# Dense products of 512 columns put into each slot of the first three attentions of a vision tower

## The chip, the cores and the metric

The kernel runs on one core of one Trainium2 chip. The metric is the device time of one execution in microseconds (us). The kernel before was timed three times: 1929.55 us is the median, 1923.34 us the lowest and 1930.13 us the highest.

## The reference, cut to what matters

32 images become 37 tokens each (36 patches and a class token) of 192 numbers. Then come seven attentions with 12 heads and five feed-forward layers, three of which send tokens to experts. The change touches the first three attentions alone, which have heads of 16 numbers. Each computes, in float32,

```
qkv = xn @ qkv_w.T                       # q, k, v: [B, 12, 37, 16]
attn = q @ k^T * scale                   # first: minus 0.2 * sum of its 8 neighbours; second: causal mask
out = softmax(attn) @ v                  # third: the diagonal is masked
h = layernorm(h + out [@ w_proj + ...])  # the first has no output projection
```

None of these values changes.

## The kernel before, in words

The 32 images are taken in 11 groups of three (`G = 11`, 111 tokens: `TG`). A program in Python (`PROGRAM`) lists steps of all stages in one order, and each engine walks the same list and does its part of each step; so the order of work on each engine is written out by hand. The stages are: attention `NEIGH`, attention `CAUSAL`, an expert layer, attention `DIAG`, then four times a wider attention (`T5`) and a feed-forward layer.

The first three attentions have `short` set. Their order comes from `short_order` (and `short_fill`, which places the small jobs): slot n of an attention holds, in this order,

- S(n): scores of group n on TensorE (`att_step`, kind "S", L1058 to L1090). First PE waits until both score banks of the slot before have been taken by VectorE. In `CAUSAL` and `DIAG` a bfloat16 product puts the mask into each bank (L1074). Then come 12 products (24 in `NEIGH`, which adds those of the neighbour sums) of 37 columns over 64 rows (L1085). In the profile a float32 product is two instructions.
- OT(n-2): the attention output of group n-2 is turned (L1140), into a projection bank, after a wait until VectorE has divided it. `NEIGH` has no OT.
- PT(n-1): the probabilities of group n-1 are turned into `ps_pt` (`turn_prob`, L992 to L1000), after waits until ScalarE has made their exponentials and has taken the turned ones of the group before.
- Y(n-2): output projection (L1157). `NEIGH` has XA in its place, which is no work of TensorE.
- E(n), exponentials, on ScalarE; PV(n-1): probabilities times values (L1119), 12 products of 51 columns.
- in between: projections QK of a later block of groups (L1034), V of the next group (L1048; in `NEIGH` also a product of one row, L1053), turns A of normalised rows (L977, in `DIAG` L971 and L973), tokens TOK (L1015), and for the follower the expert logits L (L1174) and counts CNT (L1182, L1183).

QK, V and A steps of kind fp32r (`w1_hi`, `w1_lo`, `xa_hi`, ...) run in one instruction per product. The weights of each stage lie in `w1_hi`, a ring of three slots (`W_RING`); attention a's are in slot `LOAD0[("att", a)] % W_RING`. ScalarE rounds a new load into a slot at a step W1 (L1362), after the last projection that reads the slot's old content.

VectorE (DVE) does the softmax's maximum and shift (L1550, L1552), the division (L1561, L1564), residual additions and the start of each norm; GpSimd (POOL) does the rest of the norm (L1417 to L1460) and the DMAs of rows to and from the experts (L1385); ScalarE (ACT) does exponentials and most evictions (L1332, L1338, L1310), and in `NEIGH` it spreads the queries by head (QS, L1247), which S of a block's first group waits for.

Of the kernel before, what the change touches and what calls it, by code (L numbers as in the profile page):

```python
# [25 lines left out]
G = -(-B // IPG)  # L26
# [26 lines left out]
NEIGH, CAUSAL, DIAG, T5 = 0, 1, 2, 3  # L53
# [26 lines left out]
ATTS = [Att(a) for a in range(NATT)]  # L80
# [48 lines left out]
LOADS, LOAD0 = [], {}  # L129
# [454 lines left out]
W_RING = 3  # L584
# [3 lines left out]
def tower(nc, patches, tok_w, consts, young, rows, gains, gates_w, head_scale, bias_src, wo_all, w1_all, w2_all, out, rows_in, rows_out):  # L588
    with ExitStack() as ctx:
# [29 lines left out]
        w1_hi = sb("w1_hi", [128, W_RING, 2, F], F32R)  # L619
# [68 lines left out]
        ps_pt = ps("ps_pt", [128, 512])  # L688
# [249 lines left out]
        def _(pe):  # L938
# [53 lines left out]
            def turn_prob(a, g, u):  # L992
                n = unit(a, g, u)
                pe.wait_ge(prob_ready, n + 1)
                if n:
                    pe.wait_ge(pt_taken, n)
                for i in range(4 if ATTS[a].short else 3):
                    src = short_ring(prob, n)[:, i * TG:(i + 1) * TG] if ATTS[a].short else prob[:, n % 4, i, :]
                    last = pe.transpose(ps_pt[0:TG, i * TG:(i + 1) * TG], src, ident)  # L999
                last.then_inc(pt_full, 1)  # L1000

            def att_step(st, step):
                a = st[1]
# [3 lines left out]
                kind, g = step[0], step[1]  # L1007
# [3 lines left out]
                elif kind == "TOK":  # L1011
                    bank = proj_bank(key)
# [5 lines left out]
                elif kind == "QK":  # L1018
                    _, b, j = step
# [36 lines left out]
                elif kind == "S":  # L1056
                    p = step[2]
                    banks = [score_bank((*key, e)) for e in range(2)]  # L1058
                    b = BLOCK_OF[g]
                    if g == BLOCKS[b][0] and p == 0:  # L1060

                        for j in (s.qk - 2, s.qk - 1):
                            proj_out((st, "QK", b, j))
                        if a == NEIGH:

                            pe.wait_ge(qs_ready, 4 * (b + 1))
                            pe.wait_ge(band_done, 2 * (b + 1))
                    t0 = (g - BLOCKS[b][0]) * TP
                    if s.short:
                        if SCORE[(*key, 0)] % 2:  # L1070
                            banks.reverse()
                        for bank in banks:
                            if a != NEIGH:
                                pe.matmul(bank[0:TG, 0:2 * TG], identb[:],  # L1074
                                          maskb[:, a, 0:2, :].rearrange("p h k -> p (h k)"),
                                          start=True, stop=False, skip_group_check=True)
                        parts = [(short_q(b % 2), short_k(b % 2))]
                        if a == NEIGH:
                            parts.append((qband[:, b % 2, :, :, :, :], neigh_kb(b % 2)))
                        for j in range(2):  # L1080
                            for i in range(IPG):
                                for part, (q_t, k_t) in enumerate(parts):
                                    for e, bank in enumerate(banks):
                                        at, col = 64 * e, (j * IPG + i) * NTOK
                                        ins = pe.matmul(bank[0:TG, col:col + NTOK],  # L1085
                                                        q_t[at:at + 64, j, g - BLOCKS[b][0], i, :],
                                                        k_t[at:at + 64, j, t0 + i * NTOK:t0 + (i + 1) * NTOK],
                                                        start=(a == NEIGH and part == 0),
                                                        stop=(part == len(parts) - 1), skip_group_check=True)
                                        if (j, i, part) == (1, IPG - 1, len(parts) - 1):  # L1090
                                            ins.then_inc(score_full, 1)
                        return
                    for i in range(3):
                        for e, bank in enumerate(banks):
                            c, at = s.heads(2 * p + e)[i]
                            ins = pe.matmul(bank[0:TG, i * TG:(i + 1) * TG],  # L1096
                                            qk[at:at + 64, b % 2, c, t0:t0 + TG],
                                            qk[at:at + 64, b % 2, s.chunks + c, t0:t0 + TG],
                                            start=True, stop=True, skip_group_check=True)
                            if i == 2:  # L1100
                                ins.then_inc(score_full, 1)
                elif kind == "PT":
                    turn_prob(a, g, step[2])
                elif kind == "PV":
                    p = step[2]
                    n = OUT_AT[(a, g, p)]
                    pe.wait_ge(pt_taken, unit(a, g, 0 if s.short else 2 * p + 1) + 1)
                    pe.wait_ge(o_ready, OUT_AT[(a, g - 1, p)] + 1 if s.t5 and g else n)
                    if p == 0 or s.short:
                        for j in range(s.vparts):  # L1110
                            proj_out((st, "V", g, j))
                    if s.short:
                        turned_p = short_ring(probt, unit(a, g, 0))
                        wide = VWIDE // H
                        for h in range(H):

                            at = (h // 3 % 2 * 2 + h // 6) * TG + h % 3 * NTOK
                            col = h % 6 * wide
                            last = pe.matmul(ps_o[0:NTOK, h // 6, col:col + wide], turned_p[:, at:at + NTOK],  # L1119
                                             vimg[:, g % 2, h * wide:(h + 1) * wide], start=True, stop=True,  # L1120
                                             skip_group_check=True)
                        last.then_inc(o_full, 1)
                        return
                    for e in range(2):
                        u = 2 * p + e
                        for i, (c, at) in enumerate(s.heads(u)):
                            h = s.head(c, at)
                            col = (h % 6) * (s.d + 1)
                            last = pe.matmul(ps_o[0:TG, h // 6, col:col + s.d + 1], probt[:, unit(a, g, u) % 4, i, :],  # L1129
                                             v64[:, g % 3, h, :], start=True, stop=True, skip_group_check=True)  # L1130
                    last.then_inc(o_full, 1)
                elif kind == "OT":
                    bank = proj_bank(key)
                    j = step[2]
                    pe.wait_ge(o_ready, OUT_AT[(a, g, j if s.t5 else 1)] + 1)
                    if s.short:
                        for c, n in ((0, 128), (1, 64)):
                            for i in range(IPG):
                                at = c * TG + i * NTOK
                                last = pe.transpose(bank[0:n, at:at + NTOK],  # L1140
                                                    o[0:NTOK, g % 2, i * C + c * 128:i * C + c * 128 + n],
                                                    ident[0:NTOK, 0:NTOK])
                    else:
                        for i in range(3):
                            c = 3 * j + i
                            last = pe.transpose(bank[:, i * TG:(i + 1) * TG], o[:, g % 2, c * 128:(c + 1) * 128], ident)
                    last.then_inc(proj_full, 1)
                elif kind == "Y":
                    bank = proj_bank(key)
                    for j in range(s.vparts):  # L1150
                        proj_out((st, "OT", g, j))
                    if g == 0:
                        pe.wait_ge(wo_in, 16 * a)
                    w = wo[:].rearrange("p (c n) -> p c n", c=FC)
                    parts = [(c, 128) for c in range(6)] if s.t5 else [(0, 128), (1, 64)]
                    for c, n in parts:
                        last = pe.matmul(bank[0:TG, 0:C], ot[0:n, g % 2, c, :], w[0:n, c, :],  # L1157
                                         start=(c == 0), stop=(c == len(parts) - 1))
                    last.then_inc(proj_full, 1)
# [846 lines left out]
```

## Time and profile before

| what | value |
|---|---|
| median of three runs | 1929.55 us |
| the profiled execution's own time | 1929.32 us |
| its span, first to last instruction | 1927.5 us |
| mean granted TensorE clock over the span | 0.855 |
| `NEIGH`, first scores to `CAUSAL`'s first scores | 52.6 to 195.3 us |
| `CAUSAL`, second slot to last slot's scores | 207.8 to 302.2 us |
| `DIAG`, second slot to last slot's scores | 486.2 to 581.0 us |

The granted clock is a share of full speed: TensorE runs at 2.4 GHz where it is 1.00 and at 1.2 GHz where it is 0.50; a stretch with a value between had both. Times in the views are counted from the start of the span. A slot runs from one group's scores to the next group's.

### The profile page before, as it was taken

The numbers are of one execution on the slowest core, as the hardware profiler recorded it, in microseconds if no ns is written. First come the engines' busy times: TensorE is split into PE (matmuls) and PEld (weight loads), VectorE is DVE, ScalarE is ACT, GpSimd is POOL, SyncE is SP. The second block draws the span as 40 slices with busy tenths as digits, with TensorE's granted clock in tenths as the row PEclk, the third lists the DMA queues.
The fourth block names the chain that finished last, engine by engine and source line by source line (L and its number), as shares of the span: only waits on it lengthen the run. The fifth ranks groups of instructions, "written<-read, shape, count | busy, mean of one in ns | idle before, by whom it ended". The sixth has DMA issues, their size and how long they took to land.

```text
span 1927.5 us, 33597 instructions
## 1 busy us (share of the span) xinstructions
PE 1611.0 (84%) x11901; PEld 1489.6 (77%) x11901; DVE 1066.9 (55%) x2975; ACT 776.8 (40%) x1843; POOL 549.6 (29%) x1292
## 2 busy tenths in 40 slices
PE   5888798793989998999978999588989998899970
PEld 5777676792777997988878889588888987788960
DVE  4564457232655676567764343377755668434436
ACT  1433432341343553454433444244534544254420
POOL 2244335004754112612340000453234123300030
PEclk8765766896577998999888999879989989899995
DMA  4120101451069000100014666200010000256630
GB/s 143 33 73 10 43 17 38 126 164 56 26 202 275 30 2 17 62 2 6 16 34 147 213 196 198 71 15 1 1 62 18 1 16 15 63 184 209 204 91 28
DMA packets 78393, 149.75 MB, mean 78 GB/s; under 512 B 6340, under 2 KB 57843, under 8 KB 78230
## 3 DMA queue, kind: packets, MB, share of 16 engines
q1 hardware_dynamic: 71894, 135.35, 21.9%
q0 software_dynamic: 6336, 12.26, 2.2%
q8 instruction: 98, 1.61, 0.4%
q14 instruction: 65, 0.53, 0.1%
HBM read 106.59 MB, written 41.05 MB: 77 GB/s over the span
## 4 chain that ended last, share of the span: by engine, by line
PE 51%; issue 18%; DVE 15%; DMA 6%; ACT 5%; POOL 3%; SPq 1%; another core or an unknown queue 0%; DVEq 0%; POOLq 0%; ACTq 0%
PE ps_proj L1034 10%; PE ps_proj L1157 5%; PE ps_score L1228 5%; PE ps_proj L1048 5%; PE ps_o L1129 4%; PE ps_pt L999 4%; DMA w_in<-w_all_dram 4%; PE ps_proj L1211 4%; PE ps_score L1085 3%; PE ps_score L1096 3%; PE ps_o L1119 3%; ACT w_hi L1362 2%; PE ps_proj L1015 1%; DVE prob L1536 1%; DVE w_lo L1697 1%
## 5 line engine op out<-in xcount | busy, mean ns | idle before, releaser
L1228 PE MATMUL ps_score<-w,hid 128*112 128x192 f32 (+2 forms) x1680 | 305.1, 334 | 8.9 <-DVE x L1847 8.9
L1228 PEld LDWEIGHTS ps_score<-w,hid 128*112 128x112 f32 (+2 forms) x1680 | 277.0, 180 | 11.3 <-DVE x L1847 10.8
L1352 ACT ACTIVATE hid<-ps_proj 128x224 f32<-128x224 f32 (+2 forms) x360 | 133.6, 382 | 265.7 <-PE ps_proj L1211 258.9
L1440 POOL TENSOR_SCALAR tmp<-rs,var 111x1 f32<-111x1 f32 x110 | 40.9, 372 | 583.8 <-DVE rs L1510 583.0
L1401 POOL DMA_INDIRECT tin<-rows_out,idx x66 | 68.1, 1032 | 484.9 <-issue 379.9
L999 PE MATMUL ps_pt<-const,prob 111*111 111x111 f32 x660 | 129.3, 315 | 34.2 <-ACT probt L1340 22.4
L1157 PE MATMUL ps_proj<-wo,ot 128*111 128x192 f32 (+1 forms) x616 | 138.9, 375 | 4.0 <-ACT ot L1318 3.7
L999 PEld LDWEIGHTS ps_pt<-const,prob 111*111 111x111 f32 x660 | 96.2, 205 | 55.0 <-issue 27.2
L1340 ACT ACTIVATE probt<-ps_pt 111x333 f32<-111x333 f32 x176 | 78.9, 448 | 131.1 <-PE ps_pt L999 130.5
L1129 PEld LDWEIGHTS ps_o<-v,probt 111*111 111x111 f32 x1056 | 128.9, 195 | 0.5
L1332 ACT ACTIVATE prob<-prob 111x333 f32<-111x333 f32 (+1 forms) x209 | 102.6, 493 | 58.6 <-DVE prob L1539 40.0
L1129 PE MATMUL ps_o<-v,probt 111*111 111x65 f32 x1056 | 125.6, 274 | 0.0
L1157 PEld LDWEIGHTS ps_proj<-wo,ot 128*111 128x111 f32 (+1 forms) x616 | 112.1, 203 | 15.1 <-issue 12.3
L1211 PE MATMUL ps_proj<-ta_hi,w_hi 128*128 128x224 f32 (+1 forms) x264 | 94.6, 358 | 28.6 <-ACT hid L1352 23.4
L1362 ACT ACTIVATE w_hi<-w_in 128x1536 fp32r<-128x1536 f32 x65 | 96.4, 1483 | 54.3 <-DMA w_in<-w_all_dram 54.3
L1255 ACT ACTIVATE xa_hi<-ps_turn,gainf 128x111 fp32r<-128x111 f32 x132 | 46.5, 352 | 175.7 <-PE ps_turn L977 121.9
L1285 ACT ACTIVATE qk<-ps_proj 128x336 f32<-128x336 f32 (+1 forms) x192 | 82.3, 429 | 82.6 <-PE ps_proj L1034 80.2
L1536 DVE TENSOR_TENSOR prob<-ps_score,relbias 111x333 f32<-111x333 f32 x176 | 88.8, 505 | 41.6 <-PE ps_score L1096 35.8
L1697 DVE TENSOR_TENSOR w_lo<-w_in,w_hi 128x768 fp32r<-128x768 f32 x65 | 62.3, 959 | 88.1 <-ACT w_hi L1362 87.8
L1034 PE MATMUL ps_proj<-xa_hi,w_hi 128*128 128x336 f32 (+1 forms) x240 | 91.1, 380 | 11.7 <-DVE xb L1677 8.6
L977 PE MATMUL ps_turn<-const,xn 111*128 111x111 f32 x242 | 52.1, 303 | 55.8 <-POOL xn L1460 25.7
L1539 DVE TENSOR_TENSOR prob<-prob,negmax 111x333 f32<-111x333 f32 x176 | 89.9, 511 | 6.0
(250 smaller groups left out, 4172.1 us busy)
## 6 DMA issues: line engine op xcount, KB each, us to landing
w_in<-w_all_dram SPq DMA_DIRECT2D x65, 768.0 KB, 4.3
w<-w_all_dram SPq DMA_DIRECT2D x50, 576.0 KB, 5.0
rows_in<-zero SPq DMA_DIRECT2D x1, 12320.0 KB, 47.8
rows_out<-zero SPq DMA_DIRECT2D x1, 9240.0 KB, 80.5
tin<-rows_in SPq DMA_DIRECT2D x36, 224.0 KB
rows_out<-tout SPq DMA_DIRECT2D x36, 168.0 KB
patch<-patches_dram SPq DMA_DIRECT2D x11, 333.0 KB, 3.0
wo<-wo_all_dram SPq DMA_DIRECT2D x6, 576.0 KB, 3.8
```

Of the source, the lines that this page charges most:

```text
L999: last = pe.transpose(ps_pt[0:TG, i * TG:(i + 1) * TG], src, ident)
L1034: last = pe.matmul(bank[:, 0:n * TP], w[:, slot, c, at:at + 128], src, start=(i == 0), stop=(i == len(terms) - 1))
L1048: last = pe.matmul(bank[0:TG, 0:s.vwide], src[:, g, 0:TG], w[:, slot, c, at:at + s.vwide], start=(i == 0), stop=(i == len(terms) - 1 and a ...
L1129: last = pe.matmul(ps_o[0:TG, h // 6, col:col + s.d + 1], probt[:, unit(a, g, u) % 4, i, :], v64[:, g % 3, h, :], start=True, stop=True, s ...
L1157: last = pe.matmul(bank[0:TG, 0:C], ot[0:n, g % 2, c, :], w[0:n, c, :], start=(c == 0), stop=(c == len(parts) - 1))
L1211: last = pe.matmul(bank[:, 0:width], w[:, slot, c, m * 128:(m + 1) * 128], src, start=(n == 0), stop=(n == len(terms) - 1))
L1228: last = pe.matmul(bank[0:n, 0:C], hid[:, i % 2, m, at:at + n], w2[:, slot, m, :], start=(m == 0), stop=(m == FC - 1))
L1332: act.activation(p, p, ACT.Exp).then_inc(prob_ready, 1)
L1352: act.activation(hid[:, i % 2, m, 0:n], bank[:, 0:n], ACT.Relu if b.tile is None else ACT.Gelu).then_inc(taken, 1)
L1362: act.activation(w1_hi[:, r % W_RING, :, :], w1_in[:], ACT.Copy).then_inc(w1_rounded, 1)
L1536: tell(dve.tensor_tensor(dst, scores, relbias[0:TG, 3 * u:3 * u + 3, :], ALU.add), taken, value)
L1539: ins = dve.tensor_tensor(dst, scores, negmax[:, 0:3].unsqueeze(2).to_broadcast([TG, 3, TG]), ALU.add)
```

## The change

A helper `dense` puts two products into a bank that the next real work of the same step overwrites. They take weights that are in SBUF anyway: 128 stationary columns and 512 moving columns of the attention's own `w1_hi` slot, fp32r. It is called in three places of a slot: ahead of the scores (into the first score bank, behind the waits of S), ahead of the turned probabilities (into `ps_pt`, behind the waits of PT), and ahead of the output turn (into the projection bank, behind the wait for the bank and ahead of the wait for the divided output). In `DIAG` groups above 8 have none. Nothing reads the results.

```diff
@@ turn_prob
                 if n:
                     pe.wait_ge(pt_taken, n)
+                dense(a, g, ps_pt)
                 for i in range(4 if ATTS[a].short else 3):
...
+            def dense(a, g, bank):
+
+                if not ATTS[a].short or g >= G or a == DIAG and g > 8:
+                    return
+                full = w1_hi[:, LOAD0[("att", a)] % W_RING, :, :].rearrange("p c n -> p (c n)")
+                for _ in range(2):
+                    pe.matmul(bank[:, 0:512], full[:, 0:128], full[:, 0:512], start=True, stop=True,
+                              skip_group_check=True)
@@ att_step, kind "S"
                         if SCORE[(*key, 0)] % 2:
                             banks.reverse()
+                        dense(a, g, banks[0])
                         for bank in banks:
@@ att_step, kind "OT"
                     bank = proj_bank(key)
                     j = step[2]
+                    dense(a, g, bank)
                     pe.wait_ge(o_ready, OUT_AT[(a, g, j if s.t5 else 1)] + 1)
```

## Rows read from the trace of the kernel before

**Rows 1.** The page, its first part: busy us, share of the span, instructions.
```profile
PE 1611.0 (84%) x11901; PEld 1489.6 (77%) x11901; DVE 1066.9 (55%) x2975; ACT 776.8 (40%) x1843; POOL 549.6 (29%) x1292
```

**Rows 2.** The page, its second part, in 40 slices of 48.2 us, in tenths.
```profile
PE   5888798793989998999978999588989998899970
...
PEclk8765766896577998999888999879989989899995
```

**Rows 3.** Windows: stretch, length, busy PE, PEld, DVE, ACT, POOL, clock, DMA, GB/s.
```profile
52.60:195.30 142.70, 123.33 (x1073) 110.93 (x1074) 77.25 (x211) 54.15 (x132) 54.83 (x162) 0.67 0.13 37
207.80:302.20 94.40, 87.14 (x750) 74.79 (x749) 53.56 (x184) 39.37 (x110) 31.20 (x70) 0.72 0.07 24
486.20:581.00 94.80, 87.70 (x713) 72.11 (x712) 60.58 (x169) 39.42 (x106) 63.41 (x162) 0.66 0.40 125
302.20:320.00 17.80, 16.27 (x125) 13.63 (x125) 14.25 (x58) 5.09 (x16) 11.51 (x26) 0.58 0.10 30
581.00:592.00 11.00, 11.00 (x75) 9.81 (x75) 5.99 (x15) 4.17 (x10) 5.85 (x15) 0.51 0.83 254
364.00:400.00 36.00, 36.00 (x246) 36.00 (x245) 15.46 (x26) 16.85 (x32) 0.00 (x0) 1.00 0.52 169
```

**Rows 4.** Windows: single slots of CAUSAL and DIAG, same columns.
```profile
218.00:225.30 7.30, 7.30 (x82) 5.99 (x81) 3.14 (x9) 3.98 (x11) 1.15 (x4) 1.00 0.01 2
...
268.20:282.00 13.80, 13.75 (x93) 12.06 (x92) 6.60 (x27) 4.90 (x15) 4.89 (x10) 0.50 0.05 16
...
295.40:302.20 6.80, 6.68 (x83) 5.57 (x82) 5.30 (x23) 2.22 (x8) 2.53 (x4) 1.00 0.09 26
518.90:528.90 10.00, 10.00 (x77) 8.40 (x76) 7.24 (x23) 2.63 (x9) 7.99 (x24) 0.50 0.00 0
```

**Rows 5.** Timeline of PE in CAUSAL at 1.2 GHz: start, us, what, count.
```profile
245.33 0.48 PE L1034 MATMUL ps_proj<-xb,w_hi 128*128 128x336 f32 x1
245.61 0.48 PE L1034 MATMUL ps_proj<-xb,w_lo 128*128 128x336 f32 x1
...
246.79 0.48 PE L1034 MATMUL ps_proj<-xb,w_hi 128*128 128x336 f32 x1
247.07 0.36 PE L1034 MATMUL ps_proj<-xb,w_lo 128*128 128x336 f32 x1
```
```profile
268.18 2.45 PE L1085 MATMUL ps_score<-qk 64*111 64x37 f32 x24
...
274.65 2.26 PE L1119 MATMUL ps_o<-vimg,probt 111*37 111x51 f32 x24
```

**Rows 6.** Timeline of PE in CAUSAL at 2.4 GHz.
```profile
247.74 1.36 PE L1085 MATMUL ps_score<-qk 64*111 64x37 f32 x24
249.03 0.42 PE L1034 MATMUL ps_proj<-xa_hi,w_hi 128*128 128x336 f32 x1
...
249.45 0.32 PE L1034 MATMUL ps_proj<-xa_hi,w_lo 128*128 128x336 f32 x1
249.60 0.32 PE L1034 MATMUL ps_proj<-xb,w_hi 128*128 128x336 f32 x1
...
253.40 1.30 PE L1119 MATMUL ps_o<-vimg,probt 111*37 111x51 f32 x24
```

**Rows 7.** Waits of PE in the stretches NEIGH, CAUSAL, DIAG: us, times, longest.
```profile
PE ps_score L1085 <- ACT qband L1247: 12.1, 4, 4.2
PE ps_o L1119 <- ACT probt L1338: 4.3, 5, 2.2
```
```profile
PE ps_turn L977 <- POOL xn L1460: 3.0, 1, 3.0
PE ps_turn L977 <- DVE xb L1677: 2.0, 1, 2.0
```
```profile
PE ps_turn L977 <- DVE xb L1677: 2.2, 1, 2.2
PE ps_proj L1140 <- DVE o L1564: 0.6, 1, 0.6
```

**Rows 8.** Timeline of PE around two long waits, NEIGH and CAUSAL.
```profile
89.29 0.39 PE L1085 MATMUL ps_score<-qk 64*111 64x37 f32 x4 [2.72 <-ACT qband L1247]
```
```profile
266.62 0.60 PE L977 MATMUL ps_turn<-const,xn 111*128 111x111 f32 x2 [3.03 <-POOL xn L1460]
```

## The prediction

> **What bounds the kernel now.** I read the page first. Over the span TensorE (PE) is busy 84%, DVE 55% [rows 1], and in the slices with the first three attentions (slices 2 to 7 and 11 to 13) the PE row still shows mostly 7 to 9 while the clock row beneath it shows 5 to 7 [rows 2]: the engine is occupied but slow. Then the windows of the three stretches. In NEIGH PE is busy 123.33 of 142.70 us at a mean granted clock of 0.67, in CAUSAL 87.14 of 94.40 at 0.72, in DIAG 87.70 of 94.80 at 0.66 [rows 3]. No other engine is above 67% there, so PE's instruction stream sets the pace, and its clock sets how long the stream is. Single slots show it: a CAUSAL slot takes 7.30 or 6.80 us at clock 1.00 and 13.80 us at 0.50 [rows 4], the last with somewhat more in it.
>
> Why is the clock low where PE never rests? In 268.2 to 282.0 us it was busy 13.75 of 13.80 us, and at 1.2 GHz throughout [rows 4]; in 364 to 400 us, in the expert layer, it was busy 36.00 of 36.00 at 2.4 GHz [rows 3]. The first stretch is mostly products of 37 and 51 columns, the second wide projections over 128 rows. The clock also rises inside a run of wide products: the spacing of the 336-column ones is 0.28 us at 245.33 and the duration drops from 0.48 to 0.36 at 247.07 [rows 5]. So I take it that the clock falls over long runs of narrow products and rises with wide ones, and that six wide ones per slot move the balance. That is an inference from these stretches; no run yet shows it.
>
> The Trainium skill, "TensorE: Matmul & The Clock Gate", Part 1, speaks against that: it says the gate follows how busy the engine has recently been and blames idle gaps for the low clock. By it the fully busy 268.2 to 282.0 should have been at 2.4 GHz. The trace disagrees there, and agrees where PE had long waits; by the rule alone the change would only cost, a rival below.
>
> **Change part by part.** Nothing is removed and no wait, DMA or instruction of another engine is added; the queues of SP, POOL, ACT and DVE hold what they held. PE gets pairs of products: NEIGH 11 ahead of S and 11 ahead of PT; CAUSAL 11 each ahead of S, PT and OT; DIAG 9 each (groups 0 to 8). That is (22+33+27) x 2 = 164 products, one instruction each.
>
> Price of one. No row has 512 columns of this kind. The 336-column fp32r ones follow each other at 0.15 us at 2.4 GHz (249.45 to 249.60) [rows 6] and at 0.28 at 1.2 GHz [rows 5]. Scaled by 512/336 I estimate 0.23 and 0.43 us. Bounds: 0.15 from below (the narrower product's spacing), 0.48 from above at the low clock (the full duration of one); nearest are the scaled spacings. All 164 then cost 37.7 us at the high clock, 70.5 at the low one; first products of a group can cost 0.1 more (0.42 against 0.32 [rows 6]), 8 us over the 82 pairs, which I leave to the range. The skill's same page, Part 1, gives 215.7 and 426.7 ns for such products back to back, which would make the sum 35.4 or 70.0.
>
> Of this nearly all is on the path, since PE is the pace. Behind the S pair stand the scores that DVE's maximum waits for; behind the PT pair the turns that ACT's copy and then PV wait for. The OT pair stands ahead of the wait for the divided output, and that wait can hide it, but in DIAG it was 0.6 us in one time [rows 7]: I count nothing hidden by it.
>
> What comes back. Low-clock work shrinks: 24 score instructions 2.45 to 1.36 us, PV 2.26 to 1.30, projections 0.28 to 0.15 [rows 5, 6]: a factor 0.54 to 0.58; I take 0.54, since the wide groups are as many. The share of time at 1.2 GHz is 2 x (1 - clock): 0.66 in NEIGH, 0.56 in CAUSAL, 0.68 in DIAG [rows 3]. The busy time, had all of it been at 2.4 GHz, is busy x (1 - 0.46 x share): 85.9, 64.7 and 60.3 us. Idle is 19.4, 7.3 and 7.1 us. Within these stretches the added products are 44 (the first pair just ahead of it), 52 and 50: 10.1, 12.0 and 11.5 us at 2.4 GHz. With f the new share at the low clock a stretch takes idle + (busy at 2.4 + added) / (1 - 0.46 f).
>
> The new f is my choice. NEIGH gets only four products per slot, it has slots whose scores are 48 narrow instructions, and it has four waits for QS of together 12.1 us, up to 4.2 [rows 7]; during the 2.72 us wait before 89.29 the clock was lost [rows 8], and products can't prevent that. I take f = 0.40: 96.0/0.816 + 19.4 = 137.0, a gain of 5.7 us. CAUSAL keeps two long waits, 3.0 for POOL's norm and 2.0 for DVE [rows 7], part of which the later PE takes up, and the clock falls with them (the turn after the 3.03 us wait is followed by the 13.8 us slot at 0.50 [rows 8, 4]). What changes is the way back: it rises within about a slot and no longer two. f = 0.20 and 2 us less idle: 76.7/0.908 + 5.3 = 89.8, a gain of 4.6. DIAG, likewise, f = 0.20 and 1 us less idle: 71.8/0.908 + 6.1 = 85.2, a gain of 9.6.
>
> The ends of the stages. CAUSAL's last two slots (302.2 to 320) have 16.27 us of work at 0.58 [rows 3], share 0.84: 10.0 at 2.4 GHz, plus 12 products 2.8 and 1.5 idle is 14.3 for 17.8. But DVE is busy 14.25 of it and is late next; I count half less a bit, 1.5. In DIAG's last slot (581 to 592, 11.00 at 0.51) the state at entry decides: 11.0 x 0.54 + 0.5 = 6.4 if high; half of 4.6 is 2.3. CAUSAL's first slot waits for the end of NEIGH: nothing. Sum: 5.7+4.6+9.6+1.5+2.3 = 23.7 us. Against the profiled execution's own 1929.32 us, 0.2 from the median, that is 1905.6; the 0.1 us per group above would take part of it back, so I say **1907 us**.
>
> **Both ends.** All at 2.4 GHz with the old idle: 115.4, 84.0, 78.9 and both ends in full is 27+10+16+8 = 61 us less, 1868. With f as before: 157.3, 110.7, 111.6, some 48 us more plus 2 for the ends, 1979.
>
> **Rivals.**
> - *Another engine becomes the pace.* With PE faster, DVE and POOL are next: DVE is busy 5.30 of the 6.80 us slot at 2.4 GHz [rows 4], POOL 63.41 of DIAG's 94.8 [rows 3], 7.0 us per slot. The forecast slots, 89.8/9 = 10.0 and 85.2/9 = 9.5 us, stay above both, which speaks against; the long waits on chains through DVE and POOL speak for. If the idle of the three stretches grows by 15 us from 33.8, the gain is about 8: 1921 us, within 0.5%.
> - *The clock stays up nearly throughout* (f about 0.15, 0.05, 0.05): 103.1+19.4, 78.5+5.3, 73.5+6.1 = 285.9 for 331.9, with the ends 50 less: 1880 us. For it: slots without waits already keep 2.4 GHz. Against it: NEIGH's waits for QS.
> - *The pairs cost more than the clock returns*, slower than before. Place: the same three stretches, most of all NEIGH. With the old idle they break even where 244.5/(1 - 0.46 f) = 298.1, f = 0.39, against 0.63 before. If four or six wide products are too few against the narrow ones, and f stays at 0.50, they take 351.3 for 331.9: 1949 us. Against it: a single QK group lifted the clock [rows 5], and each slot now gets a comparable piece.
> - *Busyness alone decides the clock*: PE is fully busy already, f stays, 1979 us. The 13.80 us slot at 0.50 speaks clearly against [rows 4]. It is the rule of the skill's page named above.
>
> **How the numbers follow.** Forecast 0.45 (own range 1895 to 1919), all high 0.15, another engine 0.25, too few products 0.12, busyness 0.03. A measurement of this kernel tells about 0.5% (9.6 us) from no change. Faster by over that: 0.15, nearly all of 0.45 and a little of the 0.25: 0.62. Slower: most of 0.15: 0.14. The rest, 0.24, is within. The range from 1880 to 1934 holds the forecast, most of the all-high case and the case of another engine, and leaves out the slower ones and some of the deepest gain.
>
> **What would show it.** Right: 164 instructions more on PE, each spaced by about 0.23 us where the clock is 1.00; clock in the three stretches up from 0.67, 0.72, 0.66 to about 0.80, 0.90, 0.90; few busy slots left at 0.50; score groups mostly 1.36 us; stretches near 137, 90 and 85 us; everything from 620 us on unchanged but for its start. Wrong: a clock that stays under 0.75 with PE busy (too few or not what counts); a clock near 0.9 with stretches no shorter and PE's waits for DVE, ACT or POOL far over 34 us (another pace); pairs that take over 0.7 us at the high clock (price).

## The result: 0.7% slower, where 1.2% faster was forecast

The changed kernel takes 1934.05 us in the median of 12 executions (1921.22 to 1953.79); the kernel before takes 1923.35 us in the median of the 12 that stand beside it (1907.19 to 1930.13). The ratio is 1.007, its 95% interval 1.0038 to 1.0101, so it is some 13 us slower. The ratio is not the quotient of the two medians (1.0056), and it leaves out the longest execution, 1953.79 us, as a slow one. The forecast was 1907 us with a range of 1880 to 1934: it missed the sign, and the median lies just outside the range.

The profiled execution of the changed kernel took 1949.93 us (span 1948.1). It is one of five between 1946 and 1954 us; the other seven lie between 1921 and 1938. The two traces therefore differ by 20.6 us of span, more than the medians do, and what a stage shows in one trace is checked below by kernels that have the pairs in that stage alone.

The page after, its rows for PE and the clock, beside [rows 1, 2]:

```profile
PE 1639.8 (84%) x12065; PEld 1501.8 (77%) x12065; DVE 1067.6 (55%) x2975; ACT 775.9 (40%) x1843; POOL 548.2 (28%) x1292
...
PE   5889799696589898899988999688989998889970
...
PEclk8776775598698999999888999779989989899985
```

The 164 products are there (12065 for 11901 instructions). The clock row is higher in slices 3, 4 and 6 and in 10 to 13, but slices 7 and 8 now read 5 and 5 (6 and 8 before): the second half of CAUSAL and what follows it.

Windows of the changed kernel: NEIGH, CAUSAL, its last two slots, DIAG, to be read beside [rows 3] (same columns; the stretches are bounded by the same instructions):

```profile
53.50:201.10 147.60, 131.48 (x1119) 114.42 (x1119) 76.70 (x206) 54.64 (x134) 53.57 (x158) 0.74 0.12 36
...
215.20:329.10 113.90, 107.94 (x801) 89.41 (x800) 55.27 (x189) 40.22 (x112) 32.73 (x75) 0.69 0.05 17
329.10:351.80 22.70, 22.70 (x135) 17.96 (x135) 12.59 (x54) 3.55 (x11) 9.77 (x20) 0.50 0.07 20
520.20:609.50 89.30, 82.03 (x761) 64.85 (x761) 59.69 (x168) 38.61 (x105) 61.68 (x161) 0.90 0.46 145
```

NEIGH is 147.6 us for 142.7, though its clock rose from 0.67 to 0.74. CAUSAL is 113.9 for 94.4 and its clock fell from 0.72 to 0.69. Its last two slots are 22.7 for 17.8, all of it at 1.2 GHz. DIAG is 89.3 for 94.8 at 0.90 for 0.66. So the three stages did three different things. DIAG got the clock that was forecast and 5.5 of the 9.6 us. NEIGH got some clock and paid more than that gave back. CAUSAL had the low clock at least as often as before and paid for many of the products at it.

Single slots of the changed kernel, four of CAUSAL and one of DIAG, beside [rows 4]:

```profile
227.50:236.00 8.50, 8.50 (x86) 6.94 (x85) 3.50 (x10) 3.59 (x10) 1.42 (x5) 1.00 0.00 0
281.30:298.20 16.90, 16.85 (x100) 13.86 (x98) 7.17 (x29) 5.19 (x15) 4.89 (x10) 0.51 0.05 14
298.20:314.70 16.50, 16.50 (x97) 13.82 (x96) 6.89 (x28) 3.65 (x11) 4.88 (x10) 0.50 0.05 15
314.70:329.10 14.40, 14.40 (x88) 11.71 (x87) 6.85 (x28) 2.94 (x9) 4.89 (x10) 0.50 0.06 17
...
548.80:556.00 7.20, 7.20 (x81) 5.73 (x80) 6.43 (x21) 2.86 (x10) 5.84 (x17) 1.00 0.01 2
```

The first is the slot that took 7.30 us before: six products cost 1.2 us at 2.4 GHz. The second is the one that took 13.80: they cost 3.1 us at 1.2 GHz. After it two more slots, with PE busy without a break and three pairs in each, stayed at 1.2 GHz, and the second of them is the slot that took 6.80 us at 2.4 GHz before: 14.40 now. The last row is DIAG's slot that took 10.00 us at 0.50: 7.20 us at 1.00, with its six products in it.

The timeline of PE in the slot from 281.3 us shows what lies between the pairs there (the rows of L1009 are the pairs):

```profile
283.63 1.22 PE L1009 MATMUL ps_proj<-w_hi 128*128 128x512 f32 x2
284.78 0.72 PE L1152 MATMUL ps_proj<-const,o 37*128 37x37 f32 x6
285.43 1.22 PE L1009 MATMUL ps_pt<-w_hi 128*128 128x512 f32 x2
286.44 0.95 PE L1000 MATMUL ps_pt<-const,prob 111*111 111x111 f32 x4
287.18 1.75 PE L1169 MATMUL ps_proj<-wo,ot 128*111 128x192 f32 x4
```

The two second products of these pairs, shown alone:

```profile
284.22 0.63 PE L1009 MATMUL ps_proj<-w_hi 128*128 128x512 f32 x1
...
286.02 0.63 PE L1009 MATMUL ps_pt<-w_hi 128*128 128x512 f32 x1
```

The second product starts 0.59 us behind the first (283.63 to 284.22, 285.43 to 286.02), and the next work 0.42 us behind the second (286.02 to 286.44) or 0.56 us (284.22 to 284.78, ahead of the output turn). So at 1.2 GHz a pair takes 1.0 to 1.15 us of PE's time.

Waits of PE in CAUSAL's stretch of the changed kernel, beside the second part of [rows 7]:

```profile
PE ps_turn L977 <- POOL xn L1472: 2.9, 1, 2.9
PE ps_turn L977 <- DVE xb L1689: 2.0, 1, 2.0
```

They are the waits of before, 3.0 and 2.0 us. The longer slots didn't take them up. For the wait for POOL the trace before shows a reason: PE waits for a chain that itself starts from PE's work, output projection, addition on DVE, norm on POOL, then the turn at 266.62 us [rows 8]:

```profile
258.41 1.08 PE L1157 MATMUL ps_proj<-wo,ot 128*111 128x192 f32 x4 [0.17 <-DVE upto L1781]
...
260.98 0.36 DVE L1723 TENSOR_TENSOR x<-ps_proj,x 111x192 f32<-111x192 f32 x1
...
266.39 0.24 POOL L1460 COPY xn<-xn 111x64 f32<-111x64 f32 x1
```

### The profile page after: what moved, and what is told of

It reads as the page before. It is cut to its first block, busy times and chain, and to the rows that moved or that the text cites. A ratio compares the mean times of both kernels' runs of the same rounds, so it can differ in the third digit from the quotient of the medians.

```text
span 1948.1 us, 33905 instructions
## 1 busy us (share of the span) xinstructions
PE 1639.8 (84%) x12065; PEld 1501.8 (77%) x12065; DVE 1067.6 (55%) x2975; ACT 775.9 (40%) x1843; POOL 548.2 (28%) x1292
## 4 chain that ended last, share of the span: by engine, by line
PE 52%; issue 17%; DVE 15%; DMA 6%; ACT 5%; POOL 3%; SPq 1%; another core or an unknown queue 0%; DVEq 0%; POOLq 0%; ACTq 0%
PE ps_proj L1044 9%; PE ps_score L1240 5%; PE ps_proj L1169 5%; PE ps_proj L1058 5%; PE ps_o L1140 4%; PE ps_proj L1223 4%; PE ps_pt L1000 4%; DMA w_in<-w_all_dram 4%; PE ps_score L1096 3%; PE ps_score L1107 3%; PE ps_o L1130 2%; ACT w_hi L1374 2%; PE ps_proj L1025 1%; DVE prob L1548 1%; DVE prob L1551 1%
## 5 line engine op out<-in xcount | busy, mean ns | idle before, releaser
L1000 PE MATMUL ps_pt<-const,prob 111*111 111x111 f32 x660 | 123.9, 306 | 34.2 <-ACT probt L1352 22.4
```

## The experiments

Each ratio below is against executions of the kernel before that were timed beside that run (their medians lie between 1914.02 and 1927.18 us).

**One stage at a time.** Theory A explains the result by stage, rival B by luck of a trace. In `dense` the condition was the only thing edited (DIAG shown; for the others `a != CAUSAL or g >= G` and `a != NEIGH or g >= G`):

```diff
-                if not ATTS[a].short or g >= G or a == DIAG and g > 8:
+                if a != DIAG or g > 8:
```

> The pairs stand in DIAG alone (54 products), NEIGH and CAUSAL as before. Theory A (by stage): what a stage gains or loses depends on whether its clock comes back; in the trace after, DIAG's stretch had 0.90 of the clock for 0.66 and was 5.5 us shorter, or 13 us with its first and last slots. It expects DIAG alone 5 to 13 us faster than before (ratio 0.993 to 0.997), DIAG's clock 0.85 or more. Rival B (chance of one trace): the pairs cost about their price everywhere and the clock of a stage is luck; it expects DIAG alone 0 to 5 us slower and a clock in DIAG near 0.75.

> The pairs stand in CAUSAL alone (66 products). Theory A: CAUSAL holds most of the loss, since its slots with narrow logits and counts stay at 1.2 GHz with the pairs and then take 16.5 us for 13.8; it expects 10 to 25 us slower than before (ratio 1.005 to 1.013) and a clock in CAUSAL's stretch under 0.75. Rival B: luck, 3 to 8 us slower, by a clock that is up to 0.85 in the next trace.

> The pairs stand in NEIGH alone (44 products). Theory A: NEIGH's stretch had the clock at 0.74 for 0.67 and was 4.9 us longer; it expects 3 to 8 us slower than before. Rival B: the same sign, 3 to 5 us. The two part only in the stages that follow: by A CAUSAL's and DIAG's stretches look as before.

Measured against before: DIAG alone 0.9976 (0.9951 to 1.0), CAUSAL alone 1.0105 (1.007 to 1.014), NEIGH alone 1.0013 (0.999 to 1.0036). Their sum, +0.94%, fits the whole, 1.0038 to 1.0101. Some 20 us of loss are CAUSAL's. DIAG alone gives 4.6 us at the estimate, just short of theory A's 5 to 13, and its interval ends at no change. NEIGH alone can't be told from no change, where 3 to 8 us had been expected. Windows of DIAG in the first, of CAUSAL in the second, and of NEIGH and DIAG in the third:

```profile
488.20:582.90 94.70, 87.53 (x761) 69.06 (x760) 60.10 (x168) 38.75 (x105) 62.15 (x162) 0.84 0.48 148
```
```profile
207.50:308.60 101.10, 95.34 (x802) 79.44 (x801) 54.24 (x186) 40.10 (x112) 31.39 (x73) 0.79 0.06 19
```
```profile
53.10:200.10 147.00, 131.88 (x1118) 114.65 (x1118) 76.47 (x205) 54.39 (x133) 53.31 (x158) 0.72 0.12 36
...
489.20:589.70 100.50, 94.52 (x713) 77.48 (x712) 60.42 (x169) 39.67 (x106) 63.39 (x162) 0.60 0.43 134
```

DIAG's stretch with the pairs in that stage alone, 94.70 us, is no shorter than the 94.80 of the trace before, though its clock is 0.84 for 0.66. Three things follow. CAUSAL with the same pairs had 0.79 here and 0.69 in the first trace, so rival B is right that a stage's clock is partly chance. But even at 0.79 the stretch is 101.1 us for 94.4: theory A is right that CAUSAL loses. And the last row is DIAG with nothing changed in it: 100.5 us at 0.60, for 94.8 at 0.66 in [rows 3]. The clock of a stage swings by that much from trace to trace, and a stretch of a single trace is good to 5 us or so.

So the traces of all the kernels here have to be taken together. DIAG's stretch without products (five traces) takes 93.1 to 100.5 us at 0.60 to 0.68; with the pairs (six) it takes 85.4 to 95.9 us at 0.84 to 0.95: the clocks don't overlap, the lengths do, and the means differ by some 5 us. CAUSAL's stretch without products (six traces) takes 88.4 to 99.2 us at 0.67 to 0.80, below both traces with two in each place. NEIGH's without products (five) takes 137.6 to 143.5 us, with the pairs (two) 147.0 and 147.6.

**All of a slot in one place.** Theory C: the pairs are diluted by the narrow work between them. The same number ahead of the scores alone (calls in PT and OT taken out):

```diff
-                dense(a, g, ps_pt)
...
-                for _ in range(2):
+                for _ in range(4 if a == NEIGH else 6):
...
-                    dense(a, g, bank)
```

> The same number of products or nearly (NEIGH 44, CAUSAL 66, DIAG 54), but all of a slot in one place, ahead of the scores: behind PV and V, which are the widest work of a slot. Theory C (what lifts the clock is unbroken wide work, and spread pairs are diluted by the narrow work between them): the clock comes back within a slot in CAUSAL too; low-clock slots of 16.5 us vanish, CAUSAL's stretch is near 90 us, the whole 10 to 25 us faster than the changed kernel. Rival D (only the number of products in a slot counts): the same as the changed kernel, 1.005 to 1.01 of before.

It measured 1.0135 (1.0113 to 1.0157), slower than the changed kernel. CAUSAL's stretch was 103.4 us at 0.77, NEIGH's 153.1 us at 0.69, DIAG's 87.8 us at 0.91. Theory C falls: CAUSAL's stretch is not near 90 us and the whole is not faster. Rival D named 1.005 to 1.01, and the interval lies above that as well, so place matters somewhat and this one is worse. Why wasn't tested.

**Is it wide work that lifts the clock?** The same 164 products in the same places, over 32 rows of the array for 128:

```diff
-                    pe.matmul(bank[:, 0:512], full[:, 0:128], full[:, 0:512], start=True, stop=True,
+                    pe.matmul(bank[:, 0:512], full[0:32, 0:128], full[0:32, 0:512], start=True, stop=True,
```

> The changed kernel with all 164 products over 32 rows instead of 128 (their first 32 partitions), so the same instructions, columns and places, and the same time each. Theory W (wide work over the whole array is what brings the clock back): with a quarter of the array they bring nothing back; NEIGH, CAUSAL and DIAG stretches stay at about 0.67, 0.70, 0.66 or lower, DIAG's gain of 13 us is gone, the whole 15 to 35 us slower than the changed kernel. Rival (columns streamed or mere busyness decide): the same clock in DIAG as in the changed kernel, about 0.90, and the same time.

It measured 1.0522 (1.0495 to 1.055), 2012.65 us: 98 us slower than before and so some 87 us beyond the changed kernel, where theory W had expected 15 to 35. Its windows of NEIGH, CAUSAL and DIAG, and its products at either clock:

```profile
54.00:213.70 159.70, 147.69 (x1120) 122.45 (x1119) 78.13 (x211) 55.12 (x134) 53.88 (x163) 0.65 0.11 33
226.50:358.30 131.80, 126.19 (x802) 97.50 (x801) 55.25 (x189) 40.09 (x112) 32.39 (x74) 0.62 0.05 14
549.60:674.20 124.60, 119.79 (x761) 88.79 (x760) 59.69 (x167) 39.21 (x105) 61.81 (x161) 0.60 0.46 143
```
```profile
229.44 1.22 PE L1009 MATMUL ps_pt<-w_hi 32*128 32x512 f32 x2
...
241.26 0.73 PE L1009 MATMUL ps_proj<-w_hi 32*128 32x512 f32 x2
```

A pair takes as long as the one over 128 rows (1.22 us at 1.2 GHz; at 2.4 GHz 0.73, where those took 0.63 to 0.74). The products have the columns and the places of the change and PE is busy no less, yet DIAG has 0.60 for 0.90 and is 35 us longer. It isn't one trace's luck: the mean clock of the whole execution is 0.832 to 0.836 in all four executions, where the changed kernel has 0.864 to 0.884 and the kernel before beside this run 0.846 to 0.858. So the clock came back behind products over 128 rows and not behind the same ones over 32, and busyness alone doesn't set it: PE was busy 126.19 of 131.80 us at 0.62. The Trainium skill, "TensorE: Matmul & The Clock Gate", Part 1, describes the gate by how busy the engine has been; if that is read as the busy share of a profile, this run disagrees. What about the 128 rows matters wasn't separated: whether the rows, all the cells in use or the data in them.

**More or fewer of them.** CAUSAL alone with four products in each place, and DIAG alone with one:

```diff
-                for _ in range(2):
+                for _ in range(4):
```
```diff
-                for _ in range(2):
+                for _ in range(1):
```

> CAUSAL alone, four products in each place for two (132 products, 12 per slot). Theory A2 (CAUSAL was short of wide work: six are too few): the clock of its stretch is over 0.90; but each slot pays 12 x 0.22 = 2.6 us at the high clock, so the stretch is (64.7 + 24) / 0.95 + 6 = 99 us for the 94.3 of before: no gain either, 3 to 8 us slower than before, less than the 20 us of two in each place. Rival (the clock of CAUSAL is lost to its waits and no product helps): clock under 0.80, the stretch over 110 us, 25 us or more slower than before.

> DIAG alone, one product in each place for two (27). The cost at the high clock halves, from 11.5 to 5.8 us. If three per slot are enough to hold the clock, DIAG's stretch is 82 to 90 us and the whole 8 to 12 us faster than before. If they are too few, its clock is under 0.78 and the gain of the pairs in DIAG (0.24%) is gone: 0 to 4 us slower than before.

```profile
204.60:306.60 102.00, 95.05 (x852) 78.02 (x851) 54.37 (x186) 39.70 (x112) 30.75 (x73) 0.94 0.06 18
```
```profile
491.30:583.00 91.70, 83.38 (x739) 66.59 (x738) 58.66 (x165) 39.16 (x105) 60.65 (x155) 0.81 0.45 141
```

Four in each place had CAUSAL's clock at 0.94 in this trace, as theory A2 said, so its waits don't prevent that. The stretch is 102.0 us, no shorter than the 101.1 of the trace with two: the products eat what the clock gives. The time was 1.0086 (1.0054 to 1.0119), 16 us slower than before, where 3 to 8 had been expected. For two against four the intervals overlap. One product per place in DIAG measured 0.9985 (0.996 to 1.001), not to be told from before nor from two per place; its clock of 0.81 lies between the two expected cases, and the 8 to 12 us of the better one didn't come.

**Products in waits rather than in PE's path.** The longest idle times of PE in NEIGH are the four waits of S for the spread queries. Theory I puts ten products there, ahead of the wait, into a free score bank:

```diff
                         if a == NEIGH:
-
+                            fill(banks[0], 10)
                             pe.wait_ge(qs_ready, 4 * (b + 1))
```

`fill(bank, n)` issues n products as `dense` does. One kernel has these fills alone, one has them with DIAG's pairs.

> Only the ten products ahead of each of NEIGH's four waits for the spread queries; no pairs anywhere. Theory I (the fills save by filling waits and the pairs in DIAG save by themselves, the two add up): 8 to 11 us faster than before, NEIGH's stretch 130 to 136 us, CAUSAL and DIAG as before. Rival (the gain of the kernel with both came from DIAG's pairs in a lucky trace): 0 to 4 us faster.

> DIAG's pairs as in the change, none in CAUSAL; in NEIGH no pairs, but ten products ahead of the wait of S for the spread queries, once per block (40 products), where PE stood idle 12.1 us in four waits. Theory I (in NEIGH the clock is lost in those waits, and work put into them costs nothing): NEIGH's clock 0.75 or more, its stretch 130 to 138 us for 143, the whole 8 to 15 us faster than before. Rival: the waits were short where the clock was low already, the products come out late and push the scores; NEIGH's stretch is 143 to 150 us and the whole is even with or slower than DIAG's pairs alone.

Alone: 0.996 (0.9934 to 0.9986), 7.7 us at the estimate, where 8 to 11 had been expected; the upper end of its rival, 4 us, isn't excluded. With DIAG's pairs: 0.9917 (0.9886 to 0.9948), some 16 us faster than before where 8 to 15 had been expected, a version that beats both kernels. The single gains, 0.40% and 0.24%, add up to 0.64%, inside that interval. Of the second kernel, the windows of NEIGH and DIAG, the products ahead of one wait, and PE's waits in NEIGH:

```profile
50.50:183.30 132.80, 118.97 (x1105) 104.88 (x1105) 77.62 (x210) 54.22 (x133) 55.62 (x161) 0.77 0.13 40
...
478.90:564.30 85.40, 78.22 (x763) 61.95 (x762) 58.49 (x163) 38.62 (x105) 60.68 (x155) 0.95 0.43 134
```
```profile
83.84 2.55 PE L1006 MATMUL ps_score<-w_hi 128*128 128x512 f32 x10
86.43 0.39 PE L1102 MATMUL ps_score<-qk 64*111 64x37 f32 x4
...
88.59 0.37 PE L1102 MATMUL ps_score<-qk,qband 64*111 64x37 f32 x4
```
```profile
PE ps_score L1102 <- ACT qband L1265: 1.7, 1, 1.7
```

NEIGH is 132.8 us at 0.77 for 142.7 at 0.67, and this is the clearest result of all: the five traces with these fills have 128.6 to 132.8 us at 0.77 to 0.80, the five in which NEIGH is as before 137.6 to 143.5 us at 0.67 to 0.72. The wait for the queries is 1.7 us in one time, where it was 12.1 in four: ten products in 2.55 us replaced 2.72 us of idling [rows 8], and all scores behind them took 0.37 to 0.39 us. In the kernel before, the same scores slowed down 0.8 us behind the wait:

```profile
89.86 0.41 PE L1085 MATMUL ps_score<-qk,qband 64*111 64x37 f32 x4
90.06 0.59 PE L1085 MATMUL ps_score<-qk 64*111 64x37 f32 x4
```

The same at the waits where CAUSAL and DIAG begin (36 and 28 products), then also at CAUSAL's three later waits (8, 4 and 12), then those three without the 36 and 28. All stand on top of the kernel with both of the above:

```diff
+                extra = {(("att", CAUSAL), 4): (CAUSAL, 36), (("att", DIAG), 3): (DIAG, 28), (("ffn", 0), 0): (CAUSAL, 8),
+                        (("att", CAUSAL), 10): (CAUSAL, 4), (("ffn", 0), 3): (CAUSAL, 12)}
+                if (st, g) in extra:
+                    fill(ps_pt, extra[(st, g)][1], extra[(st, g)][0])
                 if st == ("att", NEIGH):
                     pe.wait_ge(xn_ready, g + 1)
```

> The kernel with the fills and DIAG's pairs, and in addition 36 products in CAUSAL's first wait (9.1 us before its fifth turn) and 28 in DIAG's (6.8 us before its fourth turn). Theory I: at 0.22 us each they fit into the waits (8.0 and 6.2 us), keep the clock up into the slots behind, whose first took 10.1 us in CAUSAL at 0.58 and would take 6 to 7: 3 to 7 us faster than the kernel without them. Rival: the clock is at 1.2 GHz there already, 36 products then take 15 us and 28 take 12 us, longer than the waits: 4 to 12 us slower than without them.

> As the last one, and 8, 4 and 12 products in CAUSAL's three later waits of 2.0, 1.1 and 3.0 us. Theory I: they cost little when the clock is high and the slots behind (13.7 and 13.8 us at 0.5) are shortened; CAUSAL's stretch 85 to 92 us for 94 to 97, 3 to 8 us faster than the kernel without them. Rival (CAUSAL's clock is lost for other reasons, its narrow logits and counts among them): no gain, or slower by up to 5 us, as the pairs were there.

> The kernel with NEIGH's fills and DIAG's pairs, plus CAUSAL's 8, 4 and 12 products ahead of its waits, without the 36 and 28 at the stage starts. Theory I: the starts gave nothing that could be measured, so it is even with the kernel that had them, ratio 0.988 to 0.992 of before, CAUSAL's stretch 80 to 90 us at 0.85 or more. Rival: the start fill is what carried the clock through CAUSAL, and without it the stretch is 94 to 97 us at 0.70 and the whole 0.991 to 0.995.

With the starts filled: 0.9948 (0.9921 to 0.9975). With all five: 0.9909 (0.9882 to 0.9936). With the three later ones only: 0.9887 (0.9857 to 0.9917), the best estimate of the study. The intervals of the first and the third lie just apart; the others overlap, with one another and with that of the kernel that they stand on. Windows of CAUSAL's first slot and its stretch in the first, and of CAUSAL in the second and third; then the 36 products:

```profile
183.10:195.50 12.40, 10.96 (x74) 8.99 (x73) 4.65 (x15) 2.67 (x10) 6.61 (x25) 1.00 0.18 54
195.50:289.70 94.20, 88.09 (x748) 75.90 (x747) 55.00 (x188) 40.72 (x115) 33.28 (x75) 0.71 0.08 26
```
```profile
192.20:274.00 81.80, 78.78 (x772) 66.44 (x771) 53.42 (x184) 40.55 (x114) 31.35 (x70) 0.90 0.09 29
```
```profile
193.60:284.80 91.20, 88.41 (x774) 74.81 (x773) 55.11 (x188) 40.17 (x114) 33.51 (x76) 0.78 0.07 25
```
```profile
185.14 8.38 PE L960 MATMUL ps_pt<-w_hi 128*128 128x512 f32 x36
```

The start fills keep the clock at 1.00 through the 9 us wait and cost nothing (12.4 us, for 12.5 before), but the slots behind don't keep it, and the 3 to 7 us expected didn't come. With the three later waits filled CAUSAL's stretch is 81.8 us at 0.90 in one trace and 91.2 at 0.78 in the other, for 94.4 before and 88.4 to 99.2 in all traces without products there: the stage in which 66 products in PE's path cost 20 us is not slowed by 24 products that stand where PE waits anyway. The third kernel's time is within the expected 0.988 to 0.992, but its stretch missed the expected 80 to 90 us at 0.85 or more. Its interval overlaps that of the kernel without CAUSAL's fills (0.9886 to 0.9948), so their own share isn't settled.

## Why the prediction was wrong, point by point

- *PE's stream sets the pace and its clock sets the stream.* Right. The formula, idle + (busy at 2.4 GHz + added) / (1 - 0.46 f), f being the share of time at 1.2 GHz, gives with the measured clocks and idle times 107.3 + 6.0 = 113.3 us for CAUSAL after (113.9 measured) and 100.9 for CAUSAL alone (101.1). For DIAG it gives 86.4 (89.3 measured) and for NEIGH 142.3 (147.6): 3 and 5 us too little, and why stays open.
- *Wide products move the clock, busyness alone doesn't.* Right for products over 128 rows: six in a slot in DIAG, twelve in CAUSAL. The products over 32 rows show it, and the rival "busyness alone decides the clock" falls as the prediction stated it. Whether few columns also keep the clock low wasn't tested.
- *Price.* Right at the high clock: 0.23 us, by the 36 in 8.38 us and by 1.2 us for six in a slot. Too small at the low clock: the slot of 13.8 us grew by 3.1, 0.52 us a product for the 0.43 forecast, and above the 0.48 that was called its upper bound. The 0.43 itself is right for a product that follows another one, 0.42 us in the rows above; what is missing is the first one of a pair, 0.59 us. The prediction had seen that first ones cost more and left this term out of its sum. The Trainium skill, "TensorE: Matmul & The Clock Gate", "Wait — 56ns, not 53.3ns?", has 426.7 and 215.7 ns for such products back to back: the rows agree with the first for the second product of a pair, and the 36 in a row, 0.233 us each, are a little above the second.
- *The new share at the low clock: the step that failed.* The prediction put it at 0.20 in CAUSAL and DIAG and 0.40 in NEIGH, because the clock "rises within about a slot and no longer two". In DIAG it was 0.20, partly by luck: over the six traces with these pairs it lies between 0.10 and 0.32, the last in the kernel with DIAG alone. In CAUSAL it was 0.62, and 0.42 in the kernel with CAUSAL alone; from 281.3 to 351.8 us five slots in a row stayed low with the pairs in them. In NEIGH it was 0.52, and 0.56 in the kernel with NEIGH alone. The one run of wide products that had lifted the clock [rows 5] was two QK groups without a gap, ten products; a pair between 37-column products is not that. The prediction took three pairs for "a comparable piece", which no row showed. Why six products in a slot were enough in DIAG and not in CAUSAL stays open.
- *Break-even.* The rival that came true is "the pairs cost more than the clock returns", chance 0.12. Its break-even share, 0.39, was computed and stands; the three measured shares weighted by length are 0.47. The rival's 0.50 gave 351.3 us for the three stretches and 1949 us in all; this trace has 350.8 and 1949.93, but most executions were shorter. What that sum should also have said is by stage. Setting each stretch equal to its length before, the same formula gives as an estimate a break-even share of 0.48 in NEIGH, 0.26 in CAUSAL and 0.39 in DIAG; measured were 0.52 and 0.56, 0.62 and 0.42, 0.20 and 0.32. Only DIAG got below its own. CAUSAL started from the highest clock of the three, so 12 us of products had the least to win. With four in each place its share was 0.12, below the 0.20 of the forecast, and it still lost: by the formula 24 us of products bring it to 96.0 us even with no low clock at all, for 94.4 before.
- *No other engine becomes the pace.* Right: 6.0 us idle in CAUSAL and 7.3 in DIAG after, for 7.3 and 7.1 before, and 16.1 for 19.4 in NEIGH. CAUSAL's two long waits, "part of which the later PE takes up", were not taken up at all.
- *The ends.* The 1.5 us gained in CAUSAL's last two slots were 4.9 us lost (22.7 for 17.8), by the same low clock; "nothing" for CAUSAL's first slot was 1.6 us lost. DIAG's last slot took 7.5 us for 11.0, a gain of 3.5 where 2.3 had been counted.
- *NEIGH's waits for QS lose the clock and products can't prevent that.* Wrong, and the best thing found: the pairs didn't, but ten products ahead of the wait did in the wait shown, and the stage's clock rose in all five traces that have them. The reading of [rows 8] was loose too: the clock fell 0.8 us behind the 2.72 us wait, not during it.

What stays open: why CAUSAL's clock stayed low with the pairs; why all six in one place was worse than three pairs; how much of a single stage's clock is chance (the same code of DIAG had 0.60 and 0.68 in two traces); and whether CAUSAL's fills add to the rest.

## What to carry to other kernels

If TensorE is busy but slow, filler products can raise its clock, but in its own path they are bought at full price, over twice that where the clock is low. Here they paid at most in one stage of three, and by 0.24%; compute the break-even share of low-clock time by stage, not over all of them. The same products put ahead of a wait, as many as fit into it, cost nothing that could be measured here, and in the waits shown the clock was still up behind them. Check such a change with each stage by itself and with many executions, since the clock of one stretch differs between traces of the same code.

## What the runs showed of the hardware that was not expected

- Products of the same columns and duration over 32 rows instead of 128 left the clock at 0.60 in DIAG where the full ones had 0.90, and the kernel with them is 98 us slower than before.
- At 1.2 GHz the second of two 512-column products starts 0.59 us behind the first, but the work behind the second one 0.42 us later; 36 in a row at 2.4 GHz take 0.233 us each.
- The same kernel's executions spread by 33 us (1921.22 to 1953.79), with mean granted clocks from 0.884 in the shortest to 0.865 in the longest.
